# A three-layer graph attention kernel: the loop over the steady turns replaced by turns written out with constant waits

## The chip, the cores and the metric

The kernel runs on one core of one Trainium2 chip. The metric is the device time of one execution in microseconds (us). It is measured three times for the kernel before; a separate execution of the same program is profiled, and all rows below come from that one.

## The reference

32 graphs of 256 nodes with 256 features each go through two blocks. Each block is a residual around graph attention, followed by a layer norm over the features:

```
x = layernorm(x + L0(x, adj))          # one head, softmax over a row of the mask, elu
x = layernorm(x + L1(adj, x))          # two layers: 4 heads of 128 with elu, then 1 head of 256
# an attention layer, in short:
Wh = x @ W
e  = leaky_relu(score_i + score_j, 0.2); e = where(mask, e, -1e9)
out = softmax(e) @ Wh
```

The kernel calls the three attention layers A (the first block), B (four heads) and C (one head, 512 inputs).

## The kernel before

A graph (a batch of the kernel, NB = 32 of them) needs far more steps than one engine can do in a row without waiting, so the work is a software pipeline over batches. In turn i, every engine works for batch i (called t0) and for the batches i-1, i-2, i-3 and i-4 (t1 to t4), each in another part of the computation. Layer A starts for t0 and ends for t1, layer B runs for t2, layer C for t3, and the last residual, norm and store are for t4. 36 turns are needed. There is no scheduler: each engine has a function `body` in which its steps stand in an order written by hand, and each step begins with waits on semaphores that count how often a step of another engine has been done. A batch t is done at a step when its semaphore has reached `t.this()`, and the batch before it at `t.last()`; transfers count in steps of 16.

`iterations` runs `body` for all turns. Before, turns 0 to 4 are written out with constants, turns 5 to 31 (27 of them) are one loop (`eng.Fori`), and turns 32 to 35 are written out again. At the head of each loop turn an engine computes the numbers that its waits need into 12 registers (six values from i-4 to i+1, and the same multiplied by 16), and `Turn` hands these registers to the waits. All five engines loop for themselves.

The steps that the prediction speaks of:

- On VectorE (DVE) the last step of `body` is `values_b(1, 0, 4, t1)`, a copy of a projection out of PSUM with a bias (L677, VB). The first two steps of the next turn are `norm_last(1, 5, t4)` (L698, y: the second half of layer C's output, scaled and added to the residual x1c, read from PSUM bank 5) and `values_b(0, 1, 0, t2)` (L677, VB). The loop's branch and register work lie between.
- On TensorE (PE) a turn starts with 24 matmuls of `project_b` (L821); then come `spread(B, 0)` (L847), `transpose_weights(A)` (L858, probA) and `spread(B, 1, 5, t2)` (L847). The last one writes PSUM bank 5, so it waits for `norm_last(1)`, and it reads both halves of VB, so it waits for `values_b(0, 1)` too. Later come eight transposes of layer B's weights (L858, probB), the second four of which wait for GpSimd's `scale(1)`, and `spread(C)` (L847, VC), which waits for a copy by ScalarE (ACT).
- On SyncE (SP), the queue that issues the transfers, `x1_to_c` (L276) copies x1b to x1c once `norm_last` has read the old one. GpSimd (POOL) then may write x1b (`keep_x1`, L359), and goes on to `scale(0)` and `scale(1)` (L367), which also wait for DVE's reciprocals (L649, rdenB).

Of the kernel before, what the change touches and what calls it, by code (L numbers as in the profile page):

```python
# [14 lines left out]
DMA = 16  # L15


class Layer:


    def __init__(self, name, heads, width, k_tiles):
        self.name = name
        self.H = heads
        self.F = width
        self.KT = k_tiles


class Turn:


    def __init__(self, i, counts=None, off=0):
        self.i, self.counts, self.off = i, counts, off
        self.at = i + off

    @property
    def first(self):
        return self.counts is None and self.at == 0

    def batch(self, lag):
        return Turn(self.i, self.counts, self.off - lag)  # L40

    def this(self, step=1):
        return (self.at + 1) * step if self.counts is None else self.counts[(self.off + 1, step)]

    def last(self, step=1):
        return self.at * step if self.counts is None else self.counts[(self.off, step)]

    @property
    def later(self):
        return self.counts is not None or self.at > 0  # L50


COUNTS = [(k, 1) for k in range(-4, 2)]
DMA_COUNTS = [(k, DMA) for k in range(-4, 2)]


def gat_kernel(nc, x, xT, adj, adjT, w0, a0, w1, asrc1, adst1, b1, w2, asrc2, adst2, b2, out):
# [10 lines left out]
    NB, N, D = x.shape  # L68
# [9 lines left out]
    with ctx:  # L78
# [113 lines left out]
        ]  # L192

        def active(t):
            return not isinstance(t.at, int) or 0 <= t.at < NB

        def settle(eng):
            eng.wait_ge(s_cst2, 1)
# [1 line left out]
        def bank_free(eng, b, s, t):  # L200
            uses = USES[b]
            k = [u[1][0] is s for u in uses].index(True)
            for back in range(1, 8 * len(uses)):
                lag, ended = uses[(k - back) % len(uses)]
                before = t.batch(lag - uses[k][0] + (len(uses) - 1 - (k - back)) // len(uses))
                if active(before):
                    for reader in ended:
                        eng.wait_ge(reader, before.this())
                    return

        def iterations(eng, body, needed):
            LAG = 4
            for i in range(LAG + 1):
                body(Turn(i))
            regs = {(k, step): eng.alloc_register(f"count{k + LAG + 1}x{step}") for k, step in needed}
            with eng.Fori(LAG + 1, NB) as i:
                counts = {}
                for k, step in needed:
                    r = regs[(k, step)]
                    eng.reg_add(r, i, k)  # L220
                    if step > 1:
                        eng.reg_mul(r, r, step)
                    counts[(k, step)] = eng.snap(r, min_val=(LAG + 1 + k) * step, max_val=(NB + k) * step)
                body(Turn(i, counts))
            for i in range(NB, NB + LAG):
                body(Turn(i))

        x_v = x.rearrange("b (n p) f -> b p n f", p=P)
# [7 lines left out]
        @block.sync  # L236
        def _(sp):
            def load_xT(t):
                if active(t):
                    if t.later:  # L240
                        for tile in range(NT):
                            sp.wait_ge(A.s_lin[tile][0], t.last())
                    sp.dma_start(xTin[:, :, :], xT_v[t.at]).then_inc(s_x, DMA)

            def load_adj(t):
                if active(t):
                    if t.later:
                        sp.wait_ge(s_gA, t.last())
                    sp.dma_start(adj_in[:, :, :], adj_v[t.at]).then_inc(s_adj, DMA)

            def load_adjT(t):
                if active(t):
                    if t.later:
                        sp.wait_ge(s_gB, t.last())
                    sp.dma_start(adjT_in[:, :, :], adjT_v[t.at]).then_inc(s_adjT, DMA)

            def load_residual(t):
                if active(t):
                    if t.later:
                        sp.wait_ge(s_t0, t.last())  # L260
                    sp.dma_start(xres[:, :, :], x_v[t.at]).then_inc(s_xr, DMA)

            def gate_to_c(t):
                if active(t):
                    sp.wait_ge(s_diag, t.this())
                    if t.later:
                        sp.wait_ge(C.s_max[0], t.last())
                    sp.dma_start(C.gate[:, :, :], B.gate[:, :, :]).then_inc(s_g2c, DMA)

            def x1_to_c(t):  # L270
                if active(t):
                    sp.wait_ge(s_x1b, t.this())
                    if t.later:
                        for s in C.s_norm:
                            sp.wait_ge(s, t.last())
                    sp.dma_start(x1c[:, :, :], x1b[:, :, :]).then_inc(s_x2c, DMA)  # L276

            def store(t):
                if active(t):
                    sp.wait_ge(C.s_ln, t.this())  # L280
                    sp.dma_start(out_v[t.at], res[:, :, :]).then_inc(s_out, DMA)

            def body(i):
                t0, t1, t2, t3, t4 = i.batch(0), i.batch(1), i.batch(2), i.batch(3), i.batch(4)
                load_adj(t0)
                load_xT(t0)
                x1_to_c(t3)
                gate_to_c(t2)
                load_adjT(t1)
                load_residual(t0)  # L290
                store(t4)

            sp.dma_start(A.W[:, :, 0, 2:D + 2], w0.rearrange("(k p) f -> p k f", p=P)).then_inc(A.s_wld, DMA)
            sp.dma_start(att0[:, :], a0.rearrange("f o -> (f o)").partition_broadcast(P)).then_inc(A.s_wld, DMA)
            iterations(sp, body, COUNTS + DMA_COUNTS)
            sp.wait_ge(s_out, DMA * NB)

        @block.gpsimd
        def _(pool):
# [81 lines left out]
            def body(i):  # L381
# [11 lines left out]
                normalise(C, t4)  # L393
                diagonal(t1)

            iterations(pool, body, COUNTS + DMA_COUNTS)

        @block.scalar
        def _(act):
# [113 lines left out]
            act.wait_ge(s_cst, 5)  # L513
            act.wait_ge(s_cst2, 1)
            act.wait_ge(s_b1, 1)
            iterations(act, body, COUNTS + DMA_COUNTS)

        @block.vector
        def _(dve):
            def score_columns(L, heads):  # L520
                dve.wait_ge(L.s_wld, L.loads * DMA)
                n_ab = 2 * L.KT * heads[0]
                for h in heads:
                    for k in range(L.KT):
                        for j in range(2):
                            if L is A:
                                v = att0[:, (1 - j) * D:(2 - j) * D]
                            elif L is B:
                                v = att1[:, j, h * L.F:(h + 1) * L.F]
                            else:  # L530
                                v = att2[:, j, :]
                            nc.vector.scalar_tensor_tensor(out=prod[:, j, 0:L.F], in0=L.W[:, k, h, 2:L.F + 2],
                                                           scalar=0.8 if j == 0 else -0.8, in1=v, op0=ALU.mult,
                                                           op1=ALU.mult, accum_out=L.W[:, k, h, j:j + 1])\
                                .then_inc(L.s_wab, 1)
                            n_ab += 1
                            if n_ab > 1:
                                dve.wait_ge(L.s_wab, n_ab - 1)
                dve.wait_ge(L.s_wab, n_ab)
# [242 lines left out]
            nc.vector.memset(b1x[:, :, 0:2], 0.0).then_inc(s_b1, 1)  # L782
            score_columns(A, (0,))
            score_columns(B, (0, 1))
            iterations(dve, body, COUNTS + DMA_COUNTS)

        @block.tensor
        def _(pe):
# [131 lines left out]
                weigh_head(3, 4, t2)  # L920
                weigh(C, 1, 5, t3)

            iterations(pe, body, COUNTS + DMA_COUNTS)


_INS = ["x", "adj", "L0_gnn_W", "L0_gnn_a", "L1_gnn_W1", "L1_gnn_att_src1", "L1_gnn_att_dst1", "L1_gnn_b1",
# [24 lines left out]
```

## Time and profile before

| | |
|---|---|
| Time, median of 3 runs | 738.02 us (737.86 to 738.05) |
| Profiled execution: its own time | 738.62 us |
| Profiled execution: span from first to last instruction | 736.9 us |
| PE busy | 661.6 us (90%) |
| DVE busy | 600.0 us (81%) |
| ACT busy | 437.5 us (59%) |
| POOL busy | 371.1 us (50%) |
| Mean granted clock of PE | 0.977 of full speed |

Busy time counts only instructions that compute; register, branch and semaphore instructions and the issue of a transfer are not in it. They run on the engine's sequencer, which a row marks by a q behind the engine's name. PEld is the weight load of PE, which lies beside its matmuls. "Idle before" a row is the time in which its engine did nothing before it, and the name behind the arrow is what ended that; "issue" means that nothing in the trace was waited for.

### The profile page before, as it was taken

What the parts mean: (1) busy time and instruction counts of PE and PEld (TensorE: products, weight loads), DVE (VectorE), ACT (ScalarE), POOL (GpSimd) and SP (SyncE); (2) the same over time, 40 slices, a digit from 0 to 9 for tenths busy, and PEclk for the clock granted to TensorE, in tenths of its full rate; (3) what the DMA queues carried; (4) which work ended last, traced back from release to release, by engine and by line L of the source; (5) the groups of instructions that cost most, each with busy time, mean ns of one, the idle gap of its engine ahead of it and who ended that gap; (6) DMA issues with size and microseconds to landing.
All of it is one profiled execution on the core that took longest, in us unless ns stands there. A gap on an engine that the chain in (4) does not pass through costs nothing. (4 is left out here: it accounts for less than half of the span.)

```text
span 736.9 us, 17753 instructions
## 1 busy us (share of the span) xinstructions
PE 661.6 (90%) x3848; PEld 567.6 (77%) x3848; DVE 600.0 (81%) x2367; ACT 437.5 (59%) x1154; POOL 371.1 (50%) x746
## 2 busy tenths in 40 slices
PE   2469999999999999999999999999999999999973
PEld 1358888888888887888888888888888888888762
DVE  2567888898888898988888989888889888888862
ACT  1235667666555676655557766555677665556651
POOL 0214456555555565545555655555566555555542
PEclk9679999999999999999999999999999999999997
DMA  7201221222222212222222122122221221221110
GB/s 211 67 21 59 80 89 56 78 93 69 81 93 93 78 64 79 93 64 85 93 93 75 57 89 93 61 88 93 93 61 67 93 91 59 93 93 64 40 45 32
DMA packets 56002, 57.49 MB, mean 78 GB/s; under 512 B 3760, under 2 KB 51504, under 8 KB 55984
## 3 DMA queue, kind: packets, MB, share of 16 engines
q1 hardware_dynamic: 53152, 55.06, 23.2%
q10 hardware_dynamic: 2832, 2.23, 1.0%
q8 instruction: 6, 0.10, 0.1%
q14 instruction: 12, 0.10, 0.0%
HBM read 36.31 MB, written 8.39 MB: 61 GB/s over the span
## 5 line engine op out<-in xcount | busy, mean ns | idle before, releaser
L437 ACT ACTIVATE probB<-probB,shiftB 128x256 f32<-128x256 f32 x256 | 127.6, 505 | 86.3 <-DVE probB L632 85.9
L367 POOL TENSOR_SCALAR probB<-probB,rdenB 128x256 f32<-128x256 f32 x256 | 119.0, 477 | 59.8 <-DVE rdenB L649 57.6
L877 PE MATMUL PS<-probTB,VB 128*128 128x256 f32 x512 | 132.1, 380 | 1.1 <-ACT probTB L448 0.9
L359 POOL TENSOR_TENSOR x1b<-x,b2p 128x512 f32<-128x512 f32 x32 | 40.8, 1274 | 171.6 <-DMA x1c<-x1b 163.5
L834 PE MATMUL PS<-WC,hidT 128*128 128x258 f32 x512 | 122.1, 381 | 2.1 <-DVE probB L632 1.4
L632 DVE SCALAR_TENSOR_TENSOR probB<-PS,VB,gatedB 128x256 f32<-128x256 f32 x256 | 108.8, 477 | 0.8
L834 PEld LDWEIGHTS PS<-WC,hidT 128*128 128x128 f32 x512 | 94.7, 190 | 15.4 <-DVE probB L632 1.7
L877 PEld LDWEIGHTS PS<-probTB,VB 128*128 128x128 f32 x512 | 92.1, 190 | 12.7 <-ACT probTB L448 1.7
L590 DVE CUSTOM_DVE_ANT_0 gatedB<-PS,gateB 128x256 f32<-128x256 f32 x256 | 95.6, 420 | 5.3 <-PE PS L847 0.7
L808 PE MATMUL PS<-WA,xTin 128*128 128x258 f32 x256 | 70.0, 399 | 12.0 <-DMA xTin<-in_x_t_dram 12.0
L448 ACT ACTIVATE probTB<-PS 128x512 f32<-128x512 f32 x128 | 76.7, 600 | 4.5 <-PE PS L858 0.9
L821 PE MATMUL PS<-WhB,inhB 128*128 128x260 f32 x256 | 75.8, 296 | 2.1 <-DVE inlB L663 2.1
L858 PE MATMUL PS<-ident,probB 128*128 128x128 f32 x512 | 74.2, 276 | 3.4 <-POOL probB L367 3.4
L821 PE MATMUL PS<-WlB,inhB 128*128 128x260 f32 x256 | 73.5, 287 | 0.0
L821 PE MATMUL PS<-WhB,inlB 128*128 128x260 f32 x256 | 73.4, 287 | 0.0
L448 ACT ACTIVATE probTA<-PS 128x512 f32<-128x512 f32 x32 | 19.1, 597 | 90.1 <-PE PS L858 90.1
L858 PEld LDWEIGHTS PS<-ident,probB 128*128 128x128 f32 x512 | 60.3, 141 | 13.6 <-issue 5.0
L866 PE MATMUL PS<-VC,probTC 128*128 128x257 f32 x256 | 69.8, 397 | 0.8 <-ACT probTC L448 0.8
L677 DVE TENSOR_TENSOR VB<-PS,b1x 128x260 f32<-128x260 f32 x128 | 53.5, 418 | 13.4 <-PE PS L821 13.2
L866 PE MATMUL PS<-VA,probTA 128*128 128x257 f32 x256 | 62.6, 388 | 1.0 <-ACT probTA L448 1.0
L808 PEld LDWEIGHTS PS<-WA,xTin 128*128 128x128 f32 x256 | 47.2, 201 | 20.0 <-issue 12.0
L866 PEld LDWEIGHTS PS<-VC,probTC 128*128 128x128 f32 x256 | 47.3, 194 | 13.2 <-issue 7.6
(90 smaller groups left out, 1363.6 us busy)
## 6 DMA issues: line engine op xcount, KB each, us to landing
adj_in<-in_adj_dram SPq DMA_DIRECT2D x32, 256.0 KB, 2.8
xTin<-in_x_t_dram SPq DMA_DIRECT2D x32, 256.0 KB, 3.0
xres<-in_x_dram SPq DMA_DIRECT2D x32, 256.0 KB, 3.0
adjT_in<-in_adj_t_dram SPq DMA_DIRECT2D x32, 256.0 KB, 2.8
x1c<-x1b SPq DMA_DIRECT2D x32, 256.0 KB, 2.3
out_dram<-res SPq DMA_DIRECT2D x32, 256.0 KB, 2.2
gateC<-gateB SPq DMA_DIRECT2D x32, 128.0 KB, 2.0
WB<-in_L_gnn_W_dram ACTq DMA_DIRECT2D x2, 256.0 KB, 6.0
```

The lines of the kernel that those rows point to most:

```text
L367: last = pool.tensor_scalar(B.prob[h][:, k, :], B.prob[h][:, k, :], B.rden[:, k, h:h + 1], 1.0, ALU.mult, ALU.mult)
L437: last = nc.scalar.activation(L.prob[h][:, k, :], L.prob[h][:, k, :], ACT.Exp, bias=L.shift[:, k, h:h + 1], accum_out=den[:, k, h:h + 1] i ...
L448: nc.scalar.activation(L.probT[h][:, :, :], PS[b][:, :].rearrange("p (k n) -> p k n", k=NT), ACT.Copy)\
L590: last = nc.vector.tensor_tensor_reduce(out=L.gated[h][:, k, :], in0=PS[b][:, (h % 2) * N:(h % 2 + 1) * N], in1=L.gate[:, k, :], scale=0.2 ...
L632: last = nc.vector.scalar_tensor_tensor(out=L.prob[h][:, k, :], in0=PS[b][:, (h % 2) * N:(h % 2 + 1) * N], scalar=L.V[:, k, h, 1:2], in1=L ...
L677: nc.vector.tensor_tensor(B.V[:, tile, hs, :], PS[b][:, 0:2 * (B.F + 2)].rearrange("p (h f) -> p h f", h=2), b1x[:, hs, :], ALU.add).then_ ...
L808: last = nc.tensor.matmul(PS[b][:, 0:D + 2], xTin[:, k, tile * P:(tile + 1) * P], A.W[:, k, 0, :], start=(k == 0), stop=(k == A.KT - 1))
L821: last = nc.tensor.matmul(PS[b][:, 0:2 * (B.F + 2)], x_[:, k, tile * P:(tile + 1) * P], w_[:, k, 2 * g:2 * (g + 1), :].rearrange("p h f -> ...
L834: last = nc.tensor.matmul(PS[b][:, 0:D + 2], hidT[:, k, tile * P:(tile + 1) * P], C.W[:, k, 0, :], start=(k == 0), stop=(k == C.KT - 1))
L858: last = nc.tensor.transpose(PS[b][:, o:o + P], L.prob[h][:, q, k * P:(k + 1) * P], ident[:, :])
L866: last = nc.tensor.matmul(PS[b][:, 0:L.F + 1], L.probT[0][:, k, u * P:(u + 1) * P], L.V[:, k, 0, 2:L.F + 3], start=(k == 0), stop=(k == NT ...
L877: last = nc.tensor.matmul(PS[b][:, o:o + N], B.V[:, k, h, 2:B.F + 2], B.probT[h][:, k, :], start=(k == 0), stop=(k == NT - 1))
```

## The change

`iterations` becomes a plain Python loop over all 36 turns, so that every turn is written out in the program. `Turn` keeps one number, and every wait is against a constant. There is no loop, no register and no branch left on any of the five engines. The steps of `body` and their order stay as they are.

```diff
 class Turn:
-    def __init__(self, i, counts=None, off=0):
-        self.i, self.counts, self.off = i, counts, off
-        self.at = i + off
+    def __init__(self, at):
+        self.at = at
+        self.first = at == 0
+        self.later = at > 0
...
     def this(self, step=1):
-        return (self.at + 1) * step if self.counts is None else self.counts[(self.off + 1, step)]
+        return (self.at + 1) * step
...
-        def iterations(eng, body, needed):
-            LAG = 4
-            for i in range(LAG + 1):
-                body(Turn(i))
-            regs = {(k, step): eng.alloc_register(f"count{k + LAG + 1}x{step}") for k, step in needed}
-            with eng.Fori(LAG + 1, NB) as i:
-                counts = {}
-                for k, step in needed:
-                    r = regs[(k, step)]
-                    eng.reg_add(r, i, k)
-                    if step > 1:
-                        eng.reg_mul(r, r, step)
-                    counts[(k, step)] = eng.snap(r, min_val=(LAG + 1 + k) * step, max_val=(NB + k) * step)
-                body(Turn(i, counts))
-            for i in range(NB, NB + LAG):
+        def iterations(body):
+            for i in range(NB + 4):
                 body(Turn(i))
```

On DVE, at the seam between turn 4 and turn 5, which before is the entry to the loop, the program before has these rows. L216 is the loop, and L220 and L222 are the additions and multiplications of its registers; the ISA rows are register work, which is done at the head of every loop turn.

```order
L698 SCALAR_TENSOR_TENSOR y<-PS,rdenC,x1c 128x256
L642 RECIPROCAL rdenC<-PS 128x1
L677 TENSOR_TENSOR VB<-PS,b1x 128x260
L216 UNCONDITIONAL_BRANCH
L216 ISA
L220 ISA x2
L222 ISA
L698 SCALAR_TENSOR_TENSOR y<-PS,rdenC,x1c 128x256
L677 TENSOR_TENSOR VB<-PS,b1x 128x260
L590 ISA gatedB,amaxB<-PS,gateB 128x256
```

The changed program has these at the same place (its line numbers are 24 lower):

```order
L674 SCALAR_TENSOR_TENSOR y<-PS,rdenC,x1c 128x256
L618 RECIPROCAL rdenC<-PS 128x1
L653 TENSOR_TENSOR VB<-PS,b1x 128x260
L674 SCALAR_TENSOR_TENSOR y<-PS,rdenC,x1c 128x256
L653 TENSOR_TENSOR VB<-PS,b1x 128x260
L566 ISA gatedB,amaxB<-PS,gateB 128x256
```

The computing rows are the same ones in the same order; four rows of loop and register work between VB and y are gone. At the end of each loop turn, the program before has this on DVE, where REGISTER_ALU counts the loop's index and the rows ahead of it are those of the loop's last steps:

```order
L698 SCALAR_TENSOR_TENSOR y<-PS,rdenC,x1c 128x256
L642 RECIPROCAL rdenC<-PS 128x1
L677 TENSOR_TENSOR VB<-PS,b1x 128x260
L216 REGISTER_ALU
L216 COMPARE_AND_BRANCH
```

In the changed program these two rows are gone too, and the first rows of the next turn stand in their place. PE's rows have its loop work at the seam of the turns as well, in front of the first L821.

## Rows read from the trace of the kernel before

**Rows 1.** Timeline of PE: start us, duration us, instruction; first matmul of turns 4, 5, 32.
```profile
84.40 0.36 PE L821 MATMUL PS<-WhB,inhB 128*128 128x260 f32 x1
...
104.73 0.36 PE L821 MATMUL PS<-WhB,inhB 128*128 128x260 f32 x1
...
675.17 0.36 PE L821 MATMUL PS<-WhB,inhB 128*128 128x260 f32 x1
```

**Rows 2.** Windows of turn 4 and a loop turn: busy us, clock, DMA share, GB/s.
```profile
core 0: us, PE busy (x) PEld busy (x) DVE busy (x) ACT busy (x) POOL busy (x), PEclk, DMA share, GB/s
84.40:104.73 20.33, 20.02 (x123) 17.48 (x121) 18.23 (x73) 13.57 (x37) 10.76 (x22) 1.00 0.15 47
210.19:231.33 21.14, 20.13 (x122) 17.45 (x121) 18.34 (x73) 13.57 (x37) 11.57 (x24) 1.00 0.24 81
```

**Rows 3.** Waits of PE, turns 6 to 31: total us, times, longest us.
```profile
PE PS L847 <- DVE y L698: 18.4, 26, 0.8
PE PS L847 <- ACT VC L427: 8.1, 26, 0.3
```

**Rows 4.** Waits of DVE, turns 6 to 31.
```profile
DVE y L698 <- issue: 25.8, 26, 1.0
```

**Rows 5.** Timeline of DVE at the seam of two loop turns.
```profile
212.73 0.41 DVE L677 TENSOR_TENSOR VB<-PS,b1x 128x260 f32<-128x260 f32 x1
214.13 0.48 DVE L698 SCALAR_TENSOR_TENSOR y<-PS,rdenC,x1c 128x256 f32<-128x256 f32 x1 [0.99 <-issue]
214.53 0.41 DVE L677 TENSOR_TENSOR VB<-PS,b1x 128x260 f32<-128x260 f32 x1
```

**Rows 6.** Timeline of DVE at the written-out seam in front of turn 4.
```profile
86.94 0.41 DVE L677 TENSOR_TENSOR VB<-PS,b1x 128x260 f32<-128x260 f32 x1
87.26 0.47 DVE L698 SCALAR_TENSOR_TENSOR y<-PS,rdenC,x1c 128x256 f32<-128x256 f32 x1
87.66 0.42 DVE L677 TENSOR_TENSOR VB<-PS,b1x 128x260 f32<-128x260 f32 x1
88.25 0.42 DVE L590 CUSTOM_DVE_ANT_0 gatedB<-PS,gateB 128x256 f32<-128x256 f32 x1 [0.18 <-PE PS L847]
```

**Rows 7.** Timeline of PE in the same loop turn.
```profile
213.75 0.60 PE L858 MATMUL PS<-ident,probA 128*128 128x128 f32 x4
215.05 0.62 PE L847 MATMUL PS<-ident,VB 128*128 128x128 f32 x4 [0.70 <-DVE y L698]
...
220.73 1.09 PE L858 MATMUL PS<-ident,probB 128*128 128x128 f32 x8
```

**Rows 8.** Timeline of PE in turn 4.
```profile
87.95 0.60 PE L858 MATMUL PS<-ident,probA 128*128 128x128 f32 x4
88.39 0.60 PE L847 MATMUL PS<-ident,VB 128*128 128x128 f32 x4
...
94.05 1.16 PE L858 MATMUL PS<-ident,probB 128*128 128x128 f32 x8
```

**Rows 9.** Lines L216 and L220 on DVE: durations ns min/median/max, first and last start.
```profile
L216 DVEq FUSED_REGOPS  x27: 204/204/204, 107.3 to 656.8; - x27
...
L216 DVEq COMPARE_BRANCH  x27: 50/56/68, 128.1 to 677.7; - x27
...
L220 DVEq FUSED_REGOPS  x54: 176/193/210, 107.5 to 657.3; - x54
```

**Rows 10.** DMA queues in turn 4: packets, MB, share of 16 engines.
```profile
q14 instruction: 3, 0.02, 0.5%
q8 instruction: 1, 0.02, 0.3%
```

**Rows 11.** DMA queues in turns 6 to 31, all that there are.
```profile
q1 hardware_dynamic: 42848, 44.31, 24.9%
```

**Rows 12.** Transfer into x1c in the 27 loop turns, us to landing.
```profile
DMA to landing us min/median/max: 2.2/2.3/2.3
```

**Rows 13.** The same transfer before 104 us, median us to landing.
```profile
x1c<-x1b SPq DMA_DIRECT2D x2, 256.0 KB, 3.6
```

**Rows 14.** Timeline of POOL in turn 4.
```profile
90.23 1.27 POOL L359 TENSOR_TENSOR x1b<-x,b2p 128x512 f32<-128x512 f32 x1 [4.89 <-DMA x1c<-x1b]
92.52 1.92 POOL L367 TENSOR_SCALAR probB<-probB,rdenB 128x256 f32<-128x256 f32 x4 [1.02 <-DVE rdenB L649]
```

More of the change, by code:

```diff
@@ L28 @@
 class Turn:
-    def __init__(self, i, counts=None, off=0):
-        self.i, self.counts, self.off = i, counts, off
-        self.at = i + off
-    @property
-    def first(self):
-        return self.counts is None and self.at == 0
+    def __init__(self, at):
+        self.at = at
+        self.first = at == 0
+        self.later = at > 0
     def batch(self, lag):
-        return Turn(self.i, self.counts, self.off - lag)
+        return Turn(self.at - lag)
     def this(self, step=1):
-        return (self.at + 1) * step if self.counts is None else self.counts[(self.off + 1, step)]
+        return (self.at + 1) * step
     def last(self, step=1):
[L46 to L54, printed above, removed]
+        return self.at * step
 def gat_kernel(nc, x, xT, adj, adjT, w0, a0, w1, asrc1, adst1, b1, w2, asrc2, adst2, b2, out):
@@ L194, in active @@
         def active(t):
-            return not isinstance(t.at, int) or 0 <= t.at < NB
+            return 0 <= t.at < NB
         def settle(eng):
@@ L294, in _ @@
             sp.dma_start(att0[:, :], a0.rearrange("f o -> (f o)").partition_broadcast(P)).then_inc(A.s_wld, DMA)
-            iterations(sp, body, COUNTS + DMA_COUNTS)
+            iterations(body)
             sp.wait_ge(s_out, DMA * NB)
@@ L394, in body @@
                 diagonal(t1)
-            iterations(pool, body, COUNTS + DMA_COUNTS)
+            iterations(body)
         @block.scalar
@@ L515, in _ @@
             act.wait_ge(s_b1, 1)
-            iterations(act, body, COUNTS + DMA_COUNTS)
+            iterations(body)
         @block.vector
@@ L784, in _ @@
             score_columns(B, (0, 1))
-            iterations(dve, body, COUNTS + DMA_COUNTS)
+            iterations(body)
         @block.tensor
@@ L921, in body @@
                 weigh(C, 1, 5, t3)
-            iterations(pe, body, COUNTS + DMA_COUNTS)
+            iterations(body)
 _INS = ["x", "adj", "L0_gnn_W", "L0_gnn_a", "L1_gnn_W1", "L1_gnn_att_src1", "L1_gnn_att_dst1", "L1_gnn_b1",
```

## The prediction

> **What bounds the kernel now.** I read the turns first. PE's first matmul of a turn stands at 84.40, 104.73 and 675.17 us for turns 4, 5 and 32 [rows 1]. So turn 4, the last one written out ahead of the loop and the first in which all five batches are active, takes 104.73 - 84.40 = 20.33 us, and the 27 loop turns take 675.17 - 104.73 = 570.44 us, 21.13 us each. The same steps, in the same order, take 0.80 us more inside the loop. That is the whole case in one comparison, and the rest of the reading is to find where the 0.80 us lie and whether turn 4 is a fair sample.
>
> The windows come next. In a loop turn of 21.14 us PE is busy for 20.13, DVE for 18.34, ACT for 13.57 and POOL for 11.57 us [rows 2]. PE sets the pace, with 1.0 us of idle time, and the granted clock is 1.00 in both windows, so the clock explains none of the difference. The waits of PE over turns 6 to 31 name all of that idle time: 18.4 us in 26 waits of spread(B, 1) for DVE's y, 0.71 us each, and 8.1 us in 26 waits of spread(C) for ACT's copy, 0.31 us each [rows 3]. The second is a round trip from PE to ACT and back, which no loop work touches. The first is a wait for DVE, and DVE in its turn stands idle for 25.8 us in 26 times ahead of that same y, with "issue" as the only reason, 0.99 us each [rows 4]. Nothing in the trace is waited for there: DVE's own sequencer is the late one.
>
> The timeline shows the place. In the loop, DVE starts VB (the last step of a turn) at 212.73 and y (the first of the next) at 214.13, 1.40 us later [rows 5]. In the written-out seam VB starts at 86.94 and y at 87.26, 0.32 us later [rows 6]. The loop costs DVE 1.08 us per turn at this place. PE starts its transposes of probA at 213.75 and spread(B, 1) at 215.05, which is 1.30 us; in turn 4 the pair is 87.95 and 88.39, 0.44 us [rows 7, 8]. So 0.86 of DVE's 1.08 us reach PE, and the other 0.22 us were slack. The release is in fact by VB of values_b(0, 1), which follows y and starts at 214.53 and ends at 214.94, 0.11 us before PE starts [rows 5, 7]; both are late for the same reason.
>
> **The change part by part.** *The loop work of DVE* goes: one branch of 56 ns, one register instruction of 204 ns, two of 193 ns [rows 9], and some smaller ones of the same kind, with gaps between. Together they are the 1.08 us above. This takes 0.86 us off PE in each of 27 turns.
>
> At this point a rule of the Trainium skill can be weighed. The rows say that the branch itself is the small part: its median is 56 ns, and the three register instructions of rows 9 alone are 204 + 2 x 193 = 590 ns. "Advanced Engine Details and Errata", section Control Flow Timing, gives a compare-and-branch about 108 ns. If the loop cost that alone, an estimate from the page would be 27 x 0.108 = 2.9 us, so 735.1 us; by the rows the branch is half of that and ten times as much lies around it.
>
> *What is late next.* In turn 4 the eight transposes of probB take 1.16 us where they take 1.09 in the loop [rows 7, 8]: their second half waits 0.07 us for POOL. This is what remains of DVE's chain. In turn 4 DVE's first maxima stand 0.18 us idle for PE [rows 6], so DVE is then started by PE and no longer by its own backlog, and the chain from there over ACT's exponent, DVE's reciprocal and POOL's scale comes out 0.07 us after PE wants it. It gives back 0.07 of the 0.86: 0.79, against 0.80 from the turn lengths. The wait for ACT's copy stays at 0.31 us.
>
> *The loop work of PE, ACT, POOL and SP* goes too, and I cost it at nothing. PE's is fetched and done while its array works through matmuls that are queued: the two waits above are all of its idle time. ACT has 7.6 us of idle time in a turn and POOL 9.6 [rows 2]. If that cover were thin, turn 4 would show it as a gain, and it is inside the 0.80. *The waits* themselves are as many as before; a constant takes the place of a register. Turn 4 has constants already, so whatever this gives is in its 20.33 us as well. *Turns 0 to 4 and 32 to 35* are unchanged.
>
> *Fetching the longer program.* This is the one cost that the change adds. The loop turns 6 to 31 have no instruction packets at all; only the data queue appears [rows 11]. Turn 4 has four: three on one queue whose share is 0.5% of 16 x 20.33 us, so 1.6 us or 0.54 us each, and one on the other with 0.3%, so 0.98 us [rows 10]. From now on every turn has about these four. In turn 4 they delayed nobody: PE's idle time there is 20.33 - 20.02 = 0.31 us, which is the wait for ACT's copy. Fetches are made ahead of need, so I take zero. The bounds are zero and, for one fetch of 0.98 us fully in PE's way per turn, 27 x 0.98 = 26.5 us.
>
> *The sum.* 27 turns at 20.33 us are 548.9 us, against 570.4: 21.5 us less. The profiled execution took 738.62 us, so its like would take 717.1. The median of the runs is 738.02, 0.60 lower, and gives 738.0 - 21.5 = 716.5 us, 2.9% less.
>
> **The rivals.** *The gain is partly given back through the copy into x1c.* In a steady turn SP has issued two loads of the next batch shortly before this copy; in turn 4 it had not, and the DMA share of that window is 0.15 against 0.24 [rows 2]. Once y comes 0.86 us earlier after PE's matmuls, the copy is issued that much deeper into these loads. It lands after 2.3 us in all 27 loop turns [rows 12], but the two copies before the loop had a median of 3.6 us [rows 13], so it can be slower. Then POOL's keep_x1 is late by 1.3 us. After keep_x1 POOL stands idle for 1.02 us until DVE's reciprocal [rows 14], so 0.3 us of it would reach scale, and PE: 27 x 0.3 = 8 us back, and 724.5 us. Against it speaks that the copy moves the same bytes after the same loads, and so should land no later than it does now, which costs 0.1 us per turn at most. I give this 12 in 100. It also covers a smaller loss of this kind anywhere else that a single written-out turn doesn't show.
>
> *Slower: the fetches are in the way.* If the sequencer of PE or DVE had to stand still for one 0.98 us fetch in each turn, the 0.80 us gained would turn into 0.18 us lost: 27 x 0.18 = 5 us more, 743 us. It decides from 0.80 us per turn on. For it: the loop's turns fetch nothing now [rows 11], so the steady state of fetching beside full DMA traffic has not been seen. Against it: four fetches per turn passed unnoticed in turn 4, and turn 4 is the faster one. 4 in 100. "Runtime: NRT & Kernel Launch", section Instruction fetch mechanics, in the Trainium skill says that the cost of crossing from one block of instructions to the next is mostly hidden, and that a taken branch to a place that isn't held forces a fetch; by the first half the trace agrees, and the second half doesn't occur here, as the loop fetches nothing.
>
> *Hardly a gain.* If the idle time ahead of y were for the greater part something that the trace doesn't name, and only the branch and its own surroundings, 0.1 us, went, the time would be 738.0 - 27 x 0.1 = 735.3 us. The seam in front of turn 4, where y follows VB without a gap, speaks against it. By the page's 108 ns this is the 735.1 above. 3 in 100. That the change doesn't do what it says is excluded: no loop row is left in the program's order.
>
> **How the numbers follow.** The likeliest case has 81 in 100. Its own range is 714.5 to 719: downwards to turns that are 0.07 us shorter, if steady turns have no wait for POOL (27 x 0.07 = 1.9 us), upwards to turns that are 0.1 us longer (the x1c copy landing when it does now). The range for 8 in 10 reaches up to the first rival: 714 to 724.5 us. A measurement of this kernel can tell about 0.2%, 1.5 us, from no change. The likeliest case, the first rival and "hardly a gain" are all faster by more; with something left for costs that I haven't thought of, that is 95 in 100 faster, 1 same and 4 slower.
>
> **What would show it.** In the profile of the changed kernel, y should start some 0.3 us after VB in every turn, with no "issue" before it; the 26 waits of PE for y should be gone and those for ACT's copy be left; probB's eight transposes should take 1.16 us in steady turns; first matmuls of turns should stand 20.3 us apart; and instruction packets should run through the whole span, some 100 more than now. The prediction is wrong if idle time named "issue" shows up on PE or DVE at places that move from turn to turn (a fetch), if the copy into x1c takes over 3 us, or if the granted clock falls below 1.00 now that PE has hardly a pause.

## The result and the profile after

The changed kernel takes 719.72 us in the median (718.88 to 720.31, 4 runs), against 738.03 for the kernel before in the same session: a ratio of 0.9751, 95% interval 0.9734 to 0.9768, so 2.5% faster. The forecast was 716.5 us, with 714 to 724.5 as its range. The direction and the place are as forecast, and the time is 3.2 us above the likeliest case, in the part of the range that belonged to the first rival. The profiled execution took 719.68 us, with a span of 717.9.

The seam of two turns on DVE in the changed kernel, in the timeline, as an example from turn 23 (lines are 24 lower than before):

```profile
476.75 0.41 DVE L653 TENSOR_TENSOR VB<-PS,b1x 128x260 f32<-128x260 f32 x1
477.07 0.48 DVE L674 SCALAR_TENSOR_TENSOR y<-PS,rdenC,x1c 128x256 f32<-128x256 f32 x1
477.47 0.42 DVE L653 TENSOR_TENSOR VB<-PS,b1x 128x260 f32<-128x260 f32 x1
478.06 0.42 DVE L566 CUSTOM_DVE_ANT_0 gatedB<-PS,gateB 128x256 f32<-128x256 f32 x1 [0.17 <-PE PS L823]
```

y follows VB after 0.32 us, as in front of turn 4 before [rows 6], instead of 1.40 [rows 5]. The waits of PE over turns 6 to 31 (total us, times, longest us) answer to [rows 3]:

```profile
PE PS L823 <- ACT VC L403: 5.8, 20, 0.3
PE PS L834 <- POOL probB L343: 3.8, 11, 0.7
```

The 18.4 us of waiting for y are gone. In their place stand 3.8 us for POOL's scale, in 11 waits of up to 0.7 us. These waits are new. DVE has new waits in the same stretch too; "issue" means that the trace shows no cause for them:

```profile
DVE probB L608 <- issue: 0.7, 2, 0.4
...
DVE probC L608 <- issue: 0.4, 1, 0.4
DVE shiftC L594 <- issue: 0.3, 1, 0.3
```

Two windows show what a slow turn and an ordinary turn look like (busy us of each engine, granted clock, DMA share, GB/s); the row of all 27 turns stands above them:

```profile
104.08:657.37 553.29, 542.40 (x3242) 470.86 (x3241) 499.86 (x1945) 367.06 (x973) 313.52 (x622) 1.00 0.27 85
...
328.75:349.81 21.06, 20.06 (x122) 17.45 (x121) 18.98 (x73) 13.68 (x37) 12.24 (x24) 1.00 0.26 82
494.54:514.88 20.34, 20.03 (x123) 17.46 (x121) 18.27 (x73) 13.58 (x37) 11.91 (x24) 1.00 0.27 85
```

The 27 turns from 104.08 to 657.37 us take 553.3 us, where 27 x 20.33 = 548.9 had been forecast: 4.4 us more. Most turns take 20.3 us. Turns 15 to 20 in a row take 20.5 to 21.1 us and turn 21 takes 20.45; these seven hold 3.3 of the 4.4 us, and some single turns (20.6 at turns 6 and 10, 20.4 at five others) hold the rest. Turn 5 starts 0.65 us earlier than before, and the part behind turn 31 is 1.1 us shorter, which takes back 1.8 of the 4.4. So the profiled execution is 2.6 us above the 717.1 of the sum.

In turns 16 to 20 the copy into x1c is late: it lands after 3.5 to 4.6 us. The DMA queues of 6.7 us in turn 16 (packets, MB, share of 16 engines), and the three transfers issued in it (us to landing):

```profile
q1 hardware_dynamic: 960, 1.05, 48.1%
q8 instruction: 1, 0.02, 1.7%
q14 instruction: 1, 0.01, 0.3%
...
adj_in<-in_adj_dram SPq DMA_DIRECT2D x1, 256.0 KB, 2.8
xTin<-in_x_t_dram SPq DMA_DIRECT2D x1, 256.0 KB, 3.0
x1c<-x1b SPq DMA_DIRECT2D x1, 256.0 KB, 4.6
```

The 16 KB packet of instructions (q8) held one of the 16 DMA engines for 1.7% of 16 x 6.7 us, 1.8 us, just while the copy was moving, and the copy landed after 4.6 us. In the same stretch of turn 23 there is no instruction packet, and the copy lands after 2.3. POOL then has no idle time left between the copy and its scale, where it had 1.02 us in turn 4 [rows 14]. Its timeline in turn 16:

```profile
336.93 1.27 POOL L335 TENSOR_TENSOR x1b<-x,b2p 128x512 f32<-128x512 f32 x1 [6.59 <-DMA x1c<-x1b]
338.18 1.83 POOL L343 TENSOR_SCALAR probB<-probB,rdenB 128x256 f32<-128x256 f32 x4
```

In turns 17 to 19 the copy lands earlier, after 3.5 to 3.7 us, and the turns are slow all the same (20.8 to 21.0 us). There the late copy takes another way, by DVE. Its step gateA starts 7.3 us into each turn, and POOL's step into x1b, which the copy releases, now falls on it. In turn 17:

```profile
357.12 1.50 DVE L539 TENSOR_SCALAR gateA<-adj_in 128x512 bf16<-128x512 int32 x1
...
357.07 1.26 POOL L335 TENSOR_TENSOR x1b<-x,b2p 128x512 f32<-128x512 f32 x1 [5.97 <-DMA x1c<-x1b]
```

gateA takes 1.50 us instead of its median of 0.42, and ends 0.3 us behind POOL's step. DVE's reciprocals, for which POOL's scale waits, come that much later.

From this trace came the theory for the experiments, which doesn't have this second way in it. (1) All of the gain is DVE's loop work ahead of y. (2) The 4.4 us that are missing go to the fetches of the longer program: 16 KB packets, taken to be PE's, and 8 KB packets, of the others, delay the copy where they fall beside it. (3) DVE pauses by itself where it comes to a new block of instructions. The rival to (2) is that the copy is late because it is now issued deeper into the two loads.

### The profile page after: what moved, and what is told of

Read it like the earlier page. It is cut to its first block and busy times, and to the rows that moved or that the text cites. A ratio compares the mean times of both kernels' runs of the same rounds, so it can differ in the third digit from the quotient of the medians.

```text
span 717.9 us, 16745 instructions
## 1 busy us (share of the span) xinstructions
PE 660.1 (92%) x3848; PEld 566.9 (79%) x3848; DVE 604.5 (84%) x2367; ACT 438.3 (61%) x1154; POOL 372.7 (52%) x746
## 5 line engine op out<-in xcount | busy, mean ns | idle before, releaser
L834 PE MATMUL PS<-ident,probB 128*128 128x128 f32 x512 | 76.8, 275 | 7.6 <-POOL probB L343 7.2
L784 PEld LDWEIGHTS PS<-WA,xTin 128*128 128x128 f32 x256 | 46.7, 198 | 18.4 <-issue 10.6
```

What stands on the lines that cost most here:

```text
L784: last = nc.tensor.matmul(PS[b][:, 0:D + 2], xTin[:, k, tile * P:(tile + 1) * P], A.W[:, k, 0, :], start=(k == 0), stop=(k == A.KT - 1))
L834: last = nc.tensor.transpose(PS[b][:, o:o + P], L.prob[h][:, q, k * P:(k + 1) * P], ident[:, :])
```

## The experiments

All are timed against the kernel before on their own chip (738.35 to 738.67 us there). "27 turns" is the time from the first matmul of turn 5 to that of turn 32 in the profiled execution; 548.9 is the forecast. That column and the last one are of one execution, which need not be a typical one: it took 741.77 us with all but DVE written out, the slowest of 12; 716.25 with all but PE written out (716.05 to 719.46 in 5 runs); 715.66 with SP and PE written out, the fastest of 5 (up to 719.61); and 727.09 with all but SP written out (722.43 to 728.85 in 6 runs).

| Kernel | median us | ratio, 95% interval | 27 turns, us | copy into x1c, us, median / max |
|---|---|---|---|---|
| before | 738.03 | | 570.4 | 2.3 / 2.3 |
| changed | 719.72 | 0.9751 (0.9734, 0.9768) | 553.3 | 2.5 / 4.6 |
| DVE alone written out | 721.40 | 0.9770 (0.9755, 0.9785) | 553.6 | 3.0 / 3.8 |
| all but DVE written out | 738.35 | 1.0001 (0.9987, 1.0014) | 574.4 | 2.3 / 4.8 |
| all but PE written out | 717.27 | 0.9719 (0.9700, 0.9737) | 550.7 | 2.4 / 3.4 |
| loops, DVE's begun elsewhere | 718.05 | 0.9723 (0.9706, 0.9740) | 550.0 | 2.9 / 3.4 |
| the same, SP written out | 715.19 | 0.9687 (0.9675, 0.9700) | 548.6 | 2.3 / 2.9 |
| the same, SP and PE written out | 716.27 | 0.9721 (0.9704, 0.9739) | 550.1 | 2.3 / 4.1 |
| all but SP written out | 724.77 | 0.9822 (0.9798, 0.9847) | 561.6 | 3.1 / 5.1 |
| changed, copy issued first | 719.48 | 0.9749 (0.9736, 0.9762) | 553.3 | 2.3 / 4.3 |
| DVE's loop holds two turns | 735.51 | 0.9959 (0.9945, 0.9972) | 567.2 | 2.8 / 3.3 |
| changed, once more | 719.29 | 0.9739 (0.9723, 0.9755) | 552.9 | 2.6 / 4.6 |

### DVE alone written out, and all but DVE

```diff
-        def iterations(eng, body, needed):
+        def iterations(eng, body, needed, written=False):
             LAG = 4
+            if written:
+                for i in range(NB + LAG):
+                    body(Turn(i))
+                return
...
-            iterations(dve, body, COUNTS + DMA_COUNTS)
+            iterations(dve, body, COUNTS + DMA_COUNTS, written=True)
```

> The kernel before with the loop written out on DVE alone; the other four engines keep their loops and registers. Theory (all of the gain is DVE's loop work ahead of y, and the 4.4 us by which the changed kernel's 27 turns exceed 27 x 20.33 come for the greater part, some 3.4 us, from PE's instruction fetches holding up the copy into x1c, the rest from DVE's own fetches): no 16 KB instruction packets in the steady turns, the copy lands after 2.3 to 2.8 us in every turn, and the time is 719.7 - 3.4 = 716.3 us, faster than the changed kernel. Rival (the copy is late because y, and so the copy, comes earlier and deeper into the two loads of the next batch): the copy is as late as in the changed kernel, up to 4.6 us, and the time is 719.7 us. Second rival (the loops of PE, ACT, POOL or SP cost something too): over 720 us.

> The reverse: PE, ACT, POOL and SP written out, DVE keeps its loop and registers. Theory (DVE's loop work is the only one on the path): DVE's 0.99 us ahead of y and PE's wait for it of 0.71 us stay, turns of 21.13 us, 738 us, within 0.3% of before; the fetches of PE delay the copy into x1c in some turns, but y is late anyway, which may cost up to 1 us. Rival (the other engines' loops have a part in the gain): under 736 us.

The pair settles (1). With DVE alone written out most of the gain is there, 721.40 us; with all the others written out and DVE's loop left, there is none, ratio 1.0001. PE's waits in turns 6 to 31 of the latter answer to [rows 3] nearly number for number:

```profile
PE PS L851 <- DVE y L702: 18.4, 26, 0.8
PE PS L851 <- ACT VC L431: 7.3, 24, 0.3
PE PS L862 <- POOL probB L371: 2.1, 3, 1.1
```

The 27 turns of that kernel's profiled execution are 4 us longer than before, 3.4 us of it in one turn that the last section looks at. But the first expectation was missed: not 716.3, but 721.40 us, no faster than the changed kernel although PE fetches nothing. The copy lands after 2.7 us at the least in every turn there. SP's timeline shows why. With its loop it puts register work between the store and the loads:

```profile
474.43 0.40 SPq L285 DMA_DIRECT2D out_dram<-res  x1
475.57 0.37 SPq L253 DMA_DIRECT2D adj_in<-in_adj_dram  x1
476.12 0.37 SPq L247 DMA_DIRECT2D xTin<-in_x_t_dram  x1
476.80 0.47 SPq L280 DMA_DIRECT2D x1c<-x1b  x1
```

In the changed kernel the same four are issued so:

```profile
475.10 0.38 SPq L257 DMA_DIRECT2D out_dram<-res  x1
475.53 0.47 SPq L225 DMA_DIRECT2D adj_in<-in_adj_dram  x1
476.10 0.45 SPq L219 DMA_DIRECT2D xTin<-in_x_t_dram  x1
477.63 0.47 SPq L252 DMA_DIRECT2D x1c<-x1b  x1
```

The first load comes 1.14 us behind the store instead of 0.43, and the copy 0.68 us behind the second load instead of 1.53, so it moves beside both loads. The rival was thus partly right: closeness to the loads costs the copy about 0.6 us. In an ordinary turn this only uses up slack, although gateA already takes 0.5 to 0.9 us there in most turns, beside POOL's step; fetches on top of it show.

### All but PE written out

> The changed kernel with one difference: PE keeps its loop and registers. PE fetches the most instructions, and its fetches are the 16 KB ones. Theory (these fetches delay the copy into x1c): the copy lands within 2.9 us in every turn, no turn is over 20.7 us, and the time is about 716.5 us. Rival (the position of the copy among the loads delays it, or the fetches of the other engines do): 719.7 us, with the stretch of turns of 20.8 to 21.1 us still there.

The edit leaves `written=True` off for PE. The stretch of late copies is gone; one copy lands after 3.4 us and three more after 2.9 to 3.0. The 16 KB packets are gone as well (one in 27 turns, against 28). The 27 turns take 550.7 us, 2.6 less than in the changed kernel, and the median is 717.27. The expectation of 716.5 us holds in the main, though not its bounds of 2.9 us for a landing and 20.7 us for a turn (the longest takes 20.73). PE's fetches cost the changed kernel 2.1 to 2.6 us, going by the 27 turns of its two profiled executions, and 1.8 us are left for the others.

Of these 1.8 us 1.0 are DVE's own pauses: turns 6, 10, 15 and 19 lose 0.18 to 0.34 us each here, although the copy lands after 2.2 to 2.5 us, and in each of them DVE pauses for 0.32 to 0.42 us with "issue" as the cause. One late copy (turn 18) costs 0.4 us. Six turns lose 0.1 us each, and I haven't looked into why; most of the others are up to 0.03 us shorter than 20.33.

### DVE's loop begun elsewhere

```diff
-            def body(i):
+            def front(i):
...
                 meanvar(C, t4)
+            def rear(i):
+                t0, t1, t2, t3, t4 = i.batch(0), i.batch(1), i.batch(2), i.batch(3), i.batch(4)
                 low_b(7, t1)
...
-            iterations(dve, body, COUNTS + DMA_COUNTS)
...
+            front(Turn(5))
...
+            with dve.Fori(5, NB - 1) as i:
...
+                rear(Turn(i, counts))
+                front(Turn(i, counts, 1))
+            rear(Turn(NB - 1))
```

> The kernel before, all five engines with loops and registers, but DVE's loop begins at another step: ahead of low_b, where DVE stands idle for 1.0 us for ACT in every turn, instead of ahead of y. DVE has 14 registers for it instead of 12. Theory (it is the place of the loop work that costs, and nothing is fetched in a loop): y follows VB after 0.3 us, PE's wait for it is gone, and the 1.1 us of loop work hide behind the wait for ACT but for 0.1 to 0.2 us, so that turns take 20.3 to 20.5 us: 716 to 721 us. Rival (loop work costs what it costs wherever it stands, for the sequencer can't do it while the engine waits): about 1.1 us per turn at the new place, which is on PE's way to project_b: 738 us or more.

No loop is taken away here; the branch and two more registers stand where DVE waits for ACT's inhB anyway. Its waits over the 27 turns have no row for y, and that for inhB is what it was:

```profile
DVE inlB L667 <- ACT inhB L477: 26.9, 27, 1.0
DVE VB L681 <- PE PS L847: 7.7, 27, 0.3
DVE gatedB L594 <- PE PS L873: 4.7, 27, 0.2
```

The loop work vanished in a wait of 1.0 us, and the time is 718.05 us, as good as with every turn written out. Every copy lands after 2.8 to 3.4 us here, as SP has its loop. The rival falls: it is the place of the loop work that costs.

### The same with SP, and with SP and PE, written out

> The kernel with DVE's loop begun ahead of low_b, plus SP written out; PE, ACT, POOL and DVE keep loops and registers. Theory (two things make the copy into x1c late: SP's own register work, which puts the two loads 0.7 us later and so right in front of the copy, and instruction fetches; here neither is left): the copy lands after 2.2 to 2.4 us in every turn, as before, all 27 turns take 20.33 us, 549 us together, and the time is about 1 us under that of the rotated loop alone, 717 us. Rival (the fetches of other engines or chance disturb the copy still): landings of 3 us and more in some turns, no faster than the rotated loop alone, 718 us.

> The same with PE written out as well, so that PE's instruction fetches of 16 KB, one per turn, are the only fetches beside SP's few. Theory (a fetch of 16 KB that falls beside the copy into x1c delays it): as PE has some 270 instructions per turn and a fetch brings 256, the fetch wanders through the turn; about 6 turns in a row, those where it falls within 1 to 6 us behind the start of the turn, have landings of 3.5 to 4.6 us and take 20.6 to 21.1 us, the others 20.33 us; the 27 turns take 2.5 to 3.5 us more than without PE's fetches. Rival (PE's fetches are harmless, and the changed kernel's slow stretch comes from many fetches together): 20.33 us in every turn and no difference to the kernel with PE's loop.

With SP written out nearly nothing is fetched (5 instruction packets in 27 turns) and the loads are early. From turn 10 on the copy lands after 2.2 to 2.3 us but for one of 2.7. All 27 turns take 20.30 to 20.33 us. The window of the 27 turns:

```profile
104.83:653.47 548.64, 540.23 (x3243) 471.01 (x3241) 495.52 (x1945) 366.35 (x973) 312.33 (x622) 1.00 0.26 84
```

and PE's only wait in them:

```profile
PE PS L873 <- ACT VC L431: 8.2, 26, 0.3
```

That is 548.6 us for a forecast of 548.9, and 715.19 us in the median. Adding PE's fetches, and nothing else, brings the late stretch back: five landings in a row of 4.1, 4.1, 4.0, 3.5 and 3.1 us, in turns of 20.57, 20.55, 20.48, 20.86 and 20.38 us. The cost is smaller than expected, 1.5 us instead of 2.5 to 3.5 (550.1 us for the 27 turns, 716.27 us in the median). By these windows PE alone costs 1.5 us and the other engines alone 1.8, and in the changed kernel both together cost 4.4. That the two make each other worse is not shown by it: this execution was the fastest of its five, and by the ratios of the table each adds 0.003 to 0.9687 and both together 0.005 to 0.006, which is no more than the sum.

One thing here doesn't fit a copy that is merely late. The landings of 4.1, 4.1 and 4.0 us cost 0.24, 0.22 and 0.15 us; that of 3.5 us costs 0.53. In that turn (19) gateA takes 1.35 us, and in the other three 0.42: a copy that lands 0.3 us ahead of gateA's start does more harm than one that lands 0.2 us behind it.

### All but SP written out

> The changed kernel but for SP, which keeps its loop and registers. Theory (SP's register work between the store and the loads takes away the distance between loads and copy): loads 1.15 us behind the store instead of 0.43, the copy lands after 2.7 to 3.1 us in ordinary turns, POOL's scale has no slack left, and every fetch beside the copy shows: 27 turns of 555 to 557 us, 722 to 723 us. Rival (SP's loop work is hidden, for SP mostly waits): 719.7 us as the changed kernel.

This is the worst of both: every fetch, and the loads right ahead of the copy. The 27 turns take 561.6 us, PE waits 11.3 us in 30 waits for POOL, and two turns take 23.8 and 23.5 us, which no theory had foreseen (see the last section). The median, 724.77, is above the 722 to 723 expected. SP's loop, which nobody waits for in the kernel before, costs 5 us when all the others are written out, and 2.9 us (718.05 against 715.19) when only DVE's has been moved.

### The copy issued ahead of the loads

```diff
             def body(i):
...
+                x1_to_c(t3)
                 load_adj(t0)
                 load_xT(t0)
-                x1_to_c(t3)
```

> The changed kernel with one difference of order on SP: x1_to_c stands ahead of load_adj and load_xT instead of behind them. Theory (the copy is late because it shares the DMA engines with two loads of 256 KB and, in some turns, with a fetch; without the loads a fetch alone costs it at most its own 1 to 1.8 us, of which 1.0 us is slack): landings of 2.0 to 2.3 us in most turns, the stretch of turns of 20.8 to 21.1 us gone, 550 to 551 us for 27 turns, about 717 us. Price to be watched: the adjacency load is issued 2.3 to 2.7 us later, at 4 us into the turn, and lands at 7 us, when DVE's gate_a wants it at 7.3. Rival (that price decides): DVE waits for the load in each turn and PE for DVE, 720 us or more.

The copy does land after 2.3 us in the median instead of 2.5, but the time is that of the changed kernel, 719.48 us. Two things were missed. With the loads behind it, the copy still lands after 2.8 to 4.3 us in some turns with a fetch. And the load's price turned up in six turns, in DVE's waits over the 27 turns:

```profile
DVE gateA L539 <- DMA adj_in<-in_adj_dram: 3.5, 6, 1.1
```

In the two worst, turns 15 and 16 (21.2 and 21.7 us), the load lands after 4.4 and 4.5 us.

So the expectation of 717 fell, and the distance from the loads is not what makes the stretch of slow turns.

### DVE's loop holds two turns

```diff
+            with dve.Fori(0, 13) as j:
...
+                    dve.reg_mul(r, j, 2)
+                    dve.reg_add(r, r, 5 + k)
...
+                body(Turn(j, counts))
+                body(Turn(j, counts, 1))
```

> The kernel before, but DVE's loop holds two turns: 13 loop turns instead of 27, turn 31 written out, 14 registers instead of 12. Theory (the price is DVE's loop work at the seam, paid once per loop turn, and no instruction is fetched in a loop that is held): y follows VB after 0.3 us in every second turn and after 1.3 to 1.7 us in the others; turns alternate between 20.3 to 20.7 and 21.1 to 21.4 us; 738.3 - 14 x 0.8 = 727 us, up to 730 with the extra registers and the late loads of SP. Rival (a body of two turns, some 280 instructions of 64 bytes, is more than the engine holds, and the jump back waits for a fetch): instruction packets in every loop turn and an idle time of 2 us and more ahead of y in every second turn, 740 us or more.

The turns alternate as expected, but between about 20.32 and 21.74 us, and the time is 735.51 and not 727. The timeline of DVE at a seam with the branch:

```profile
232.17 0.41 DVE L677 TENSOR_TENSOR VB<-PS,b1x 128x260 f32<-128x260 f32 x1
234.16 0.48 DVE L698 SCALAR_TENSOR_TENSOR y<-PS,rdenC,x1c 128x256 f32<-128x256 f32 x1 [1.58 <-issue]
```

VB to y is 1.99 us, against 1.40 [rows 5], at the same one branch. What is more is 14 multiplications by 2 and two registers with their sums. That prices the register work: some 0.6 us for these. The branch is the smaller part of the 1.08 us: from its start to that of the first register instruction it is 0.28 us, here and in the kernel before, its own 56 ns [rows 9] included. The rival falls too: one 8 KB instruction packet was fetched between 125 and 650 us, so a body of two turns is held as well.

### The changed kernel once more

> The changed kernel itself once more, on the same chip as the one above. Theory (a wandering 16 KB fetch of PE, beside the 8 KB ones, delays the copy into x1c for some turns in a row, and DVE pauses 0.3 to 0.4 us where it comes to a new block of 128 instructions with no wait to hide it): again a stretch of 4 to 8 turns with landings of 3 to 5 us and turns of 20.5 to 21.1 us, and DVE's pauses at the same instructions as in the first profile; 718 to 721 us. Rival (the slow stretch was chance): 27 turns of 20.33 to 20.6 us without a stretch, 716 to 717 us.

719.29 us, and turns 15 to 21 are the slow ones again, at 20.51 to 20.99 us, with landings of up to 4.6 us. This is no chance: a turn has a fixed number of instructions, and so the fetch falls at nearly the same place in the same turn (the 16 KB packet of turn 16 starts 4.7 us into it in the first profile and 4.9 us in this one). Turn 15 is slow by DVE's pause in both, with landings of 2.6 us. DVE's pauses recur too. Counted over the trace's records of DVE, those ahead of the instructions 703, 1217, 1984, 2495 and 3135 were 0.32, 0.32, 0.42, 0.38 and 0.18 us in the first profile, and 0.32, 0.32, 0.42, 0.38 and 0.18 us in this one; this profile has one more, of 0.43 us ahead of 2367. All these numbers are 63 to 65 above a multiple of 128. With DVE alone written out, 30 packets of 8 KB go with 3834 records of DVE in 27 turns, 128 each, so a pause falls where a packet ends. Most packet ends show no such pause. Two of the pauses of the first profile, in the timeline:

```profile
137.92 0.34 DVE L594 SCALAR_TENSOR_TENSOR shiftC<-topC,amaxC 128x2 f32<-128x2 f32 x1 [0.32 <-issue]
...
321.94 0.88 DVE L608 SCALAR_TENSOR_TENSOR probC<-PS,VC,gatedC 128x256 f32<-128x256 f32 x2 [0.42 <-issue]
```

In the kernel with DVE's loop begun elsewhere and SP written out no such pause is left in turns 6 to 31.

## Why the prediction was right, and where it was off

**What bounds the kernel, and where the loop costs**: right. y follows VB after 0.32 us, PE's wait for it is gone, and only DVE's loop matters (1.0001 with all the others written out).

**Turns of 20.33 us**: right for turns that no fetch disturbs. The kernel with neither loop work at the seam nor more than five fetches has 27 of them at 20.30 to 20.33 us.

**probB's eight transposes at 1.16 us**, with 0.07 us of waiting for POOL in them: right. In the ordinary turns 22 to 25 they take 1.17 us each.

**"Fetches are made ahead of need, so I take zero"**: this is the step that failed, and it is a term mis-sized, at 0 us instead of about 4.4. I had looked at whether an engine stood still for its instructions, and in turn 4 none did. The greater part of the cost came by another way: a 16 KB fetch occupies one DMA engine for 0.9 to 1.8 us, and the copy landed up to 2.3 us later beside it, or shortly behind it (in turn 20 the packet ends 1.0 us before the copy is issued). From there it reached PE by POOL alone (turns 16 and 20) or by POOL's step on top of DVE's gateA (turns 17 to 19); these five turns lost 3.0 us. Turn 4 could not show it, as its fetches fell elsewhere; the place wanders from turn to turn. DVE's own pause is the smaller part: turns 6, 10 and 15, with landings of 2.2 to 2.6 us, lost 0.75 us together, and some of turn 19's 0.6 us is such a pause too. It had been visible in the kernel before: one row of its last turns has 0.43 us of idle time with "issue" as its cause, ahead of probC, outside the loop. So had the late copy. The median of 3.6 us [rows 13] hides two unlike landings, 2.3 us in turn 4 and 4.9 us in turn 3, and beside the latter there is a 16 KB packet:

```profile
q8 instruction: 1, 0.02, 0.8%
...
x1c<-x1b SPq DMA_DIRECT2D x1, 256.0 KB, 4.9
```

Two of the signs that were named for the prediction being wrong did show, at places that move from turn to turn: "issue" ahead of DVE's steps, and copies of over 3 us. Instruction packets are 3 per turn, 81 in the 27 turns, where four had been counted on.

**The first rival**, the copy into x1c landing late, is what happened: it had 8 us for turns that would all be late, and five turns in a row were. That the time lies within the stated range rests on this rival's 8 us; the likeliest case alone ended at 719. Its mechanism was the wrong half, though. I named the loads; closeness to them costs 0.6 us of slack (2.9 instead of 2.3 us), and only SP's own loop makes it close. I argued as well that the copy "should land no later than it does now", which missed the fetches.

**"Slower: the fetches are in the way"** saw the right cause and for the greater part the wrong victim, an engine's sequencer. DVE's did pause, for 0.2 to 0.4 us in a few turns, not for a fetch in each.

**The loop work of SP at nothing**: right for the kernel before, wrong as a piece of this change. Without SP written out the same change gives 724.77 us.

**What lies outside the 27 turns** was taken as unchanged; it was 1.8 us shorter in the profiled execution. The start varies by up to 2.4 us among these kernels (102.8 to 105.2 us at turn 5), and I have not looked into why. No run changes only whether POOL's step meets gateA; that the one holds up the other is read from the times of the two steps, in turn after turn, and why it does is not shown.

The version that beats both is the one with DVE's loop begun ahead of low_b and SP written out, at 715.19 us: 3.1% faster than before, with a ratio whose interval (0.9675 to 0.9700) lies below that of the changed kernel.

## What to carry to other kernels

Look for idle time named "issue" ahead of an instruction that others wait for: loop work (here 1.1 us per turn, the greater part of it register arithmetic for the waits) is free at a place where the engine waits anyway, and costs all but the slack (here 0.86 of 1.08 us) at a seam that another engine waits for. Moving the loop's seam can give what unrolling gives, without the fetches that unrolling adds. When a program grows, look at whether the transfers that stand on the path by less than 1 to 2 us of slack can bear a fetch beside them, and not only at whether an engine runs out of instructions. And when a step of GpSimd moves in time, look at the durations of VectorE's steps beside it, which no row of waits shows.

## What the runs showed of the hardware

Instructions are fetched by the same DMA engines as data. A 16 KB packet takes 0.9 to 1.9 us there, and a 256 KB copy beside it took up to 4.6 us instead of 2.3 in the changed kernel (5.1 with all but SP written out). Loads are held up too: in turn 19 of the changed kernel, with the packet 3.1 us into the turn, the two loads land after 4.4 and 4.5 us, where 2.9 and 3.1 are their medians.

POOL's step into x1b (f32, 128x512) held up DVE's gateA (int32 to bf16, 128x512). Where POOL's step still had 0.2 us or more to run when gateA started, gateA took 0.5 to 1.5 us instead of 0.42 and ended 0.3 us behind it, in each of 124 turns of the twelve profiled executions: 8.81 and 8.52 us into turn 17 of the changed kernel, 8.66 and 8.38 us into turn 19 with SP and PE written out.

An idle PE can make a delay much longer. In the profiled execution of the kernel with all but DVE written out, one turn took 24.50 us instead of 21.14. PE had waited for y, as always, and then twice for POOL's scale, behind a copy that landed after 4.8 us. Its timeline there:

```profile
348.44 0.63 PE L862 MATMUL PS<-ident,probB 128*128 128x128 f32 x4 [1.06 <-POOL probB L371]
349.85 0.63 PE L862 MATMUL PS<-ident,probB 128*128 128x128 f32 x4 [0.78 <-POOL probB L371]
...
350.53 1.68 PE L812 MATMUL PS<-WA,xTin 128*128 128x258 f32 x4
352.00 1.91 PE L881 MATMUL PS<-probTB,VB 128*128 128x256 f32 x4
353.71 1.28 PE L812 MATMUL PS<-WA,xTin 128*128 128x258 f32 x4
```

The four matmuls of L812 take 1.04 us in other turns. The windows (busy us, granted clock in front of the DMA share) show the cause:

```profile
336.68:350.30 13.62, 11.07 (x70) 9.52 (x69) 11.93 (x44) 7.09 (x21) 5.53 (x11) 1.00 0.26 79
350.53:354.80 4.27, 4.27 (x14) 3.46 (x13) 3.64 (x16) 2.00 (x8) 3.02 (x8) 0.60 0.35 113
354.83:361.18 6.35, 6.35 (x39) 5.41 (x38) 3.40 (x13) 4.48 (x9) 3.10 (x7) 1.00 0.07 26
```

After these waits the granted clock fell to its lower level, 1.2 GHz: 0.60 over 4.27 us is 3.4 us at half of full speed, in which PE had no pause, and then it came back. This is about half of what that turn lost. Against an ordinary turn PE was 1.7 us behind after the waits, and the slower matmuls added 1.6 us. The two turns of 23.8 and 23.5 us in the kernel with all but SP written out have the same pattern: two waits for POOL close together, of 0.8 to 1.2 us, and then 3.4 us at 0.50. The changed kernel never got there within its 27 turns.
